# Two layers with causal attention, spectral mixing, channel attention and routed experts: affinities token by row in their own banks, six tiles routed in pairs, first expert weights copied as parts of their buffer come free

## The reference

```python
x = input_features.reshape(-1, D)
aff = jax.lax.stop_gradient(x @ centroids.T)          # 4096 x 8
eid = jnp.argmax(aff, axis=-1)
alpha = jax.nn.sigmoid(jnp.sum(x * centroids[eid], axis=-1, keepdims=True))
xn = (x - mu) * jax.lax.rsqrt(var + EPS)
xln = xn * ln_g[eid] + ln_b[eid]
for e in range(E):                                     # 8 experts, 256 -> 1024 -> 256
    h = jax.nn.relu(xln @ w1[e] + b1[e])
    ffn = ffn + onehot[:, e:e + 1] * (h @ w2[e] + b2[e])
out = x + alpha * ffn
```

## Time and profile before

| | us |
|---|---|
| median of 3 runs | 1555.1 |
| lowest and highest | 1551.25, 1556.09 |
| the profiled execution | 1549.12 |
| its span, first to last instruction | 1547.1 |
| TensorE busy | 1417.8 |
| VectorE busy | 1076.7 |
| ScalarE busy | 854.5 |
| GpSimd busy | 240.9 |

### The profile page before, as it was taken

The page is one execution under the profiler, slowest core; times in us unless marked ns, Lnnn a source line. Parts: engine busy times, 40 slices in busy tenths (PEclk is TensorE's granted clock), DMA queues, the critical chain, the costliest instruction groups (busy, mean ns, idle before and its releaser), DMA issues. The chain is left out here.

```text
span 1547.1 us, 43841 instructions
## 1 busy us (share of the span) xinstructions
PE 1417.8 (92%) x18356; PEld 858.0 (55%) x18356; DVE 1076.7 (70%) x1993; ACT 854.5 (55%) x1783; POOL 240.9 (16%) x380
## 2 busy tenths in 40 slices
PE   7878999999999999999999999898977559999998
PEld 4434444444444444444444453786754259999997
DVE  2376768888887888878888871554558647677675
ACT  2335647767677677676776767552425323433333
POOL 3212021011101111021111110000112611111111
PEclk9999999999999999999999999897998779999999
DMA  8574018513215113142300000570032254554541
GB/s 234 158 120 91 22 64 120 66 26 49 34 28 68 27 30 47 28 59 28 88 3 3 4 2 2 190 257 7 1 98 79 76 208 171 182 186 178 186 175 71
DMA packets 77823, 134.09 MB, mean 87 GB/s; under 512 B 12226, under 2 KB 64443, under 8 KB 72252
## 3 DMA queue, kind: packets, MB, share of 16 engines
q1 hardware_dynamic: 72412, 121.45, 30.4%
q0 software_dynamic: 3408, 8.43, 1.6%
q10 hardware_dynamic: 1808, 1.41, 0.3%
HBM read 67.77 MB, written 23.11 MB: 59 GB/s over the span
## 5 line engine op out<-in xcount | busy, mean ns | idle before, releaser
L1512 DVE TENSOR_REDUCE part_max<-pair 128x2 f32<-128x1024 f32 (+2 forms) x576 | 647.5, 1162 | 115.3 <-PE pair L982 57.4
L1334 ACT ACTIVATE big<-pair 128x512 f32<-128x512 f32 (+1 forms) x1120 | 565.2, 610 | 239.7 <-PE pair L1003 237.4
L976 PE MATMUL pair<-big 128*32 128x512 bf16 (+3 forms) x5120 | 359.6, 352 | 29.1 <-DVE part_max L1512 24.2
L1003 PE MATMUL pair<-big 128*32 128x512 bf16 (+3 forms) x5120 | 345.1, 351 | 3.4 <-issue 1.4
L1025 PE MATMUL pair<-big 128*17 128x512 f32 (+3 forms) x2560 | 280.3, 528 | 2.7 <-issue 2.3
L976 PEld LDWEIGHTS pair<-big 128*32 128x32 bf16 x5120 | 135.1, 97 | 198.4 <-DVE part_max L1512 98.8
L1003 PEld LDWEIGHTS pair<-big 128*32 128x32 bf16 x5120 | 126.8, 96 | 174.3 <-ACT big L1334 88.7
L1347 ACT ACTIVATE std<-moments,eps_col 128x1 f32<-128x1 f32 (+1 forms) x110 | 32.5, 295 | 261.6 <-DVE moments L1550 261.6
L1878 POOL TENSOR_SCALAR_AFFINE_SELECT big<-big 128x512 f32<-128x512 f32 x128 | 80.0, 637 | 474.3 <-ACT big L1334 474.3
L1242 PEld LDWEIGHTS pair<-big,tok 128*128 128x128 f32 x1248 | 147.8, 195 | 4.9 <-DVE big L1778 3.0
L1242 PE MATMUL pair<-big,tok 128*128 128x128 f32 x1248 | 148.3, 278 | 2.4 <-DMA tok<-big 1.4
(11 more groups left out here) (163 smaller groups left out, 1279.0 us busy)
## 6 DMA issues: line engine op xcount, KB each, us to landing
tok<-big SPq DMA_DIRECT2D x39, 1024.0 KB
big<-in_L_ffn_w SPq DMA_DIRECT2D x16, 1024.0 KB, 12.3
big<-split_dram SPq DMA_DIRECT2D x216, 64.0 KB, 4.6
split_dram<-big SPq DMA_DIRECT2D x32, 384.0 KB, 2.7
big<-split_dram SPq DMA_DIRECT2D x42, 256.0 KB, 6.1
big<-routed_dram SPq DMA_DIRECT2D x39, 129.0 KB, 2.1
tok<-in_L_attn_x SPq DMA_DIRECT2D x8, 512.0 KB, 9.2
big<-in_c_query_rows SPq DMA_DIRECT2D x8, 512.0 KB, 5.3
```

Of the source, the lines that this page charges most:

```text
L976: mm = pe.matmul(bank[q:q + STRIPE, o:o + w], m.q_op[slot][:, step.qt, h, step.r * P + q:step.r * P + q + STRIPE], m.k_op[slot][:, h, step ...
L1003: mm = pe.matmul(m.bank[step.bank][k:k + STRIPE, n * w:(n + 1) * w], m.k_op[slot][:, h, step.kb * P + k:step.kb * P + k + STRIPE], m.q_op[ ...
L1334: act.activation(m.p_ring[:, step.place, step.heads[0]:step.heads[-1] + 1, step.at:step.at + w], m.bank[step.bank][:, 0:len(step.heads) * ...
L1512: dve.tensor_reduce(m.part_max[(step.u * QT + step.qt) % 2][:, step.r, step.heads[0]:step.heads[0] + n, step.c], banks[:, :, 0:w], X, ALU. ...
```

## The change

Affinities. For each of the four blocks of a tile the turned tokens are the stationary operand and the centroids are moved, so that the result is token by row, 128 x 8 for a block. It goes to one of two banks of its own (5 and 6), and VectorE reads it there. The copy by ScalarE and the transposes are gone; the product banks are used by products alone. Counts have bank 7.

Routes. The steps Best, Hot, Choose and PlaceRows are made for a route and no more for a tile; a route is one or two tiles (`ROUTES`). A step of two tiles works on 64 values a row in place of 32; its counts take nine small products in place of five. With the rules of the plan the steps behind C5 come as: A1, F4, Best 0; C6, Hot 0; A2, Choose 0; F5, PlaceRows 0; C7; A3; F6, Best 1; A4, Hot 1; F7, Choose 1; A5 (with End of F7 ahead of it), PlaceRows 1; A6, Best 2; Hot 2, A7, Choose 2; PlaceRows 2; and then routes 3 and 4 step by step.

Weights. `scatter` is four semaphores, one for each eight blocks. SP copies the first three weights ahead of the row fetches: copy i waits for the experts' numbers and for the scatters of its own eight blocks, but not for the other scatters, the pads written by ScalarE or the rows.

```diff
+
+ROUTES = [(0, 1), (2, 3), (4, 5), (6,), (7,)]
+SCATTERS = 8
-TURN_BANKS, PRODUCT_BANKS, ROUTE_BANK, FOLD_BANKS = (0, 1), (2, 3, 4), 5, (6, 7)
+TURN_BANKS, PRODUCT_BANKS, FOLD_BANKS = (0, 1), (2, 3, 4), (6, 7)
+AFFINITY_BANKS, COUNT_BANK = (5, 6), 7
...
-            if g and g - 1 not in self.affine_turned:
+            route = next(i for i, tiles in enumerate(ROUTES) if g in tiles)
+            if route >= 2 and route - 2 not in self.made_hot:
                 self.n_job += ROUTE_LAG
-                while g - 1 not in self.affine_turned:
+                while route - 2 not in self.made_hot:
                     take(self.routes, 1)
-            b, added, affine = self.product_bank()
-            self.n_affine += 1
-            self.bank_affine[b] = self.n_affine
-            self.steps.append(Affinity(self.turn_of[stage, g], g, b, added, affine))
+            self.steps.append(Affinity(self.turn_of[stage, g], g, route))
             self.routed[self.turn_of[stage, g]] = g + 1
             self.affine_job[g] = self.n_job
...
     def route_steps(self):
-        for g in range(TILES):
-            while self.affine_job.get(g, self.n_job) + ROUTE_LAG > self.n_job:
+        for route, tiles in enumerate(ROUTES):
+            while self.affine_job.get(tiles[-1], self.n_job) + ROUTE_LAG > self.n_job:
                 yield
-            self.steps.append(Best(g))
-            self.affine_turned.add(g)
+            self.steps.append(Best(route))
             yield
-            self.steps.append(Hot(g))
+            self.steps.append(Hot(route))
+            self.made_hot.add(route)
             yield
-            self.steps.append(Choose(g))
+            self.steps.append(Choose(route))
...
+            self.steps.append(PlaceRows(route, self.norm_of["F", tiles[-1]] + 1))
             yield
...
+        self.affinity = [self.bank[b] for b in AFFINITY_BANKS]
+        self.count_all = self.bank[AFFINITY_BANKS[len(ROUTES) % 2]][:, 0:EXPERTS]
...
         elif isinstance(step, Affinity):
-            slot = step.n % 2
+            slot, tiles = step.n % 2, ROUTES[step.route]
             pe.wait_ge(s.turn_copied, 2 * step.n + 2)
-            if step.added:
-                pe.wait_ge(s.added, step.added)
-            if step.affine:
-                pe.wait_ge(s.affine_copied, step.affine)
             pe.wait_ge(s.params_set, 3)
-            for c in range(KC):
-                mm = pe.matmul(m.bank[step.bank][0:EXPERTS, :], m.cent_t[:, c, :], m.turned_x[slot][:, c, :],
-                               start=(c == 0), stop=(c == KC - 1))
+            if step.route == 1:
+                pe.wait_ge(s.channel_copied, KC * BATCHES)
+            elif step.route >= 2:
+                pe.wait_ge(s.hot_set, step.route - 1)
+            for r in range(BPT):
+                o = ((step.g - tiles[0]) * BPT + r) * EXPERTS
+                for c in range(KC):
+                    mm = pe.matmul(m.affinity[step.route % 2][:, o:o + EXPERTS], m.turned_x[slot][:, c, r * P:(r + 1) * P],
+                                   m.cent_t[:, c, :], start=(c == 0), stop=(c == KC - 1))
             mm.then_inc(s.turn_used, 1)
...
-        elif isinstance(step, Best):
-            g = step.g
-            pe.wait_ge(s.affine_copied, g + 1)
-            if g:
-                pe.wait_ge(s.counts_taken, g)
-            for i in range(BPT):
-                mm = pe.transpose(m.bank[ROUTE_BANK][:, i * EXPERTS:(i + 1) * EXPERTS], m.aff_t[:, i * P:(i + 1) * P],
-                                  m.ident[0:EXPERTS, 0:EXPERTS])
-            mm.then_inc(s.affine_turned, 1)
...
         elif isinstance(step, Hot):
+            i, blocks = step.route, len(ROUTES[step.route]) * BPT
+            n, counts, hot = blocks * EXPERTS, m.bank[COUNT_BANK], m.hot[i % 2][:, 0:blocks, :]
+            pe.wait_ge(s.hot_set, i + 1)
+            pe.wait_ge(s.chosen_set, i + 1)
+            if i == 0:
+                pe.wait_ge(s.onesb_set, 1)
+                pe.wait_ge(s.cbias_set, BATCHES)
+            else:
+                pe.wait_ge(s.counts_taken, i)
+            pe.matmul(counts[:, 0:n], m.before, hot.rearrange("p b e -> p (b e)"), start=True, stop=False)
+            for j in range(blocks - 1):
+                pe.matmul(counts[:, (j + 1) * EXPERTS:n], m.ones_b, wide(hot[:, j, :], [P, blocks - 1 - j, EXPERTS], 1),
                           start=False, stop=False)
+            pe.matmul(counts[:, 0:n], m.ones_b, wide(m.chosen[i % 2], [P, blocks, EXPERTS], 1),
                       start=False, stop=True).then_inc(s.counted, 1)
+    pe.wait_ge(s.chosen_set, len(ROUTES) + 1)
+    pe.matmul(m.count_all, m.ones_b, m.chosen[len(ROUTES) % 2], start=True, stop=True).then_inc(s.counted, 1)
...
-        elif isinstance(step, Affinity):
-            act.wait_ge(s.turn_used, step.g + 1)
-            if step.g:
-                act.wait_ge(s.affine_turned, step.g)
-            act.activation(m.aff_t, m.bank[step.bank][0:EXPERTS, :], ACTF.Copy).then_inc(s.affine_copied, 1)
...
         elif isinstance(step, Best):
+            i, tiles = step.route, ROUTES[step.route]
+            blocks, shape = slice(tiles[0] * BPT, (tiles[-1] + 1) * BPT), [P, len(tiles) * BPT, EXPERTS]
+            affinity = m.affinity[i % 2][:, 0:shape[1] * EXPERTS].rearrange("p (b e) -> p b e", e=EXPERTS)
+            if i == 0:
                 dve.wait_ge(s.channel_in, 128)
                 dve.wait_ge(s.grammed, BATCHES)
+            dve.wait_ge(s.turn_used, tiles[-1] + 1)
+            step_done(dve.tensor_reduce(m.tok[:, blocks, D], affinity, X, ALU.max))
 
         elif isinstance(step, Hot):
+            i, tiles = step.route, ROUTES[step.route]
+            blocks, shape = slice(tiles[0] * BPT, (tiles[-1] + 1) * BPT), [P, len(tiles) * BPT, EXPERTS]
+            affinity = m.affinity[i % 2][:, 0:shape[1] * EXPERTS].rearrange("p (b e) -> p b e", e=EXPERTS)
+            equal, order = m.equal[i % 2][:, 0:shape[1], :], m.order[i % 2][:, 0:shape[1]]
+            step_done(dve.tensor_tensor(equal, affinity, wide(m.tok[:, blocks, D], shape, 2), ALU.is_equal))
+            step_done(dve.tensor_tensor(equal, equal, wide(rank, shape, 1), ALU.mult))
+            step_done(dve.tensor_reduce(order, equal, X, ALU.max))
+            dve.tensor_tensor(m.hot[i % 2][:, 0:shape[1], :], wide(rank, shape, 1), wide(order, shape, 2),
                               ALU.is_equal).then_inc(s.hot_set, 1)
+            dve.wait_ge(s.hot_set, i + 1)
 
         elif isinstance(step, Choose):
+            i, n = step.route, len(ROUTES[step.route]) * BPT
+            step_done(dve.tensor_reduce(m.chosen_g, m.hot[i % 2][:, 0:n, :].rearrange("p b e -> p e b"), X, ALU.add))
+            if i:
+                dve.wait_ge(s.counted, i)
+            dve.tensor_tensor(m.chosen[(i + 1) % 2], m.chosen[i % 2], m.chosen_g, ALU.add).then_inc(s.chosen_set, 1)
+            dve.wait_ge(s.chosen_set, i + 2)
 
         elif isinstance(step, PlaceRows):
+            i, tiles = step.route, ROUTES[step.route]
+            n = len(tiles) * BPT
+            shape, place, row = [P, n, EXPERTS], m.place[i % 2][:, 0:n, :], m.row[i % 2][:, 0:n]
+            dve.wait_ge(s.counted, i + 1)
+            dve.tensor_tensor(place, m.bank[COUNT_BANK][:, 0:n * EXPERTS].rearrange("p (b e) -> p b e", e=EXPERTS),
+                              wide(region, shape, 1), ALU.add).then_inc(s.counts_taken, 1)
+            dve.wait_ge(s.counts_taken, i + 1)
+            step_done(dve.tensor_tensor(place, place, m.hot[i % 2][:, 0:n, :], ALU.mult))
+            step_done(dve.tensor_reduce(row, place, X, ALU.add))
+            dve.tensor_copy(m.position[:, tiles[0] * BPT:(tiles[-1] + 1) * BPT], row).then_inc(s.placed, 1)
+            dve.wait_ge(s.placed, i + 1)
 
...
         elif isinstance(step, PlaceRows):
-            g = step.g
-            pool.wait_ge(s.placed, g + 1)
+            tiles = ROUTES[step.route]
+            pool.wait_ge(s.placed, step.route + 1)
             pool.wait_ge(s.normed, step.normed)
-            for blk in range(g * BPT, (g + 1) * BPT):
+            for blk in range(tiles[0] * BPT, (tiles[-1] + 1) * BPT):
                 pool.indirect_dma_start(m.routed_dram, bass.IndirectOffsetOnAxis(ap=m.position[:, blk:blk + 1], axis=0),
-                                        m.tok[:, blk, :], None).then_inc(s.scatter, 16)
+                                        m.tok[:, blk, :], None).then_inc(s.scatter[blk // SCATTERS], 16)
 
...
+
+    sp.wait_ge(s.expert_set, 1)
+    sp.wait_ge(s.experts_in, 16 * 2 * EXPERTS)
+    for i in range(W1_AHEAD):
+        sp.wait_ge(s.scatter[i], 16 * SCATTERS)
+        fetch_w1(i)
     sp.wait_ge(s.rows_set, 1)
-    sp.wait_ge(s.expert_set, 1)
-    sp.wait_ge(s.scatter, 16 * BLOCKS)
+    for scatter in s.scatter:
+        sp.wait_ge(scatter, 16 * SCATTERS)
     sp.wait_ge(s.pads_out[0], 16 * EXPERTS // 2)
     sp.wait_ge(s.pads_out[1], 16 * EXPERTS // 2)
-    sp.wait_ge(s.experts_in, 16 * 2 * EXPERTS)
     for i in range(ROWS_AHEAD):
```

(2 more changed lines are left out.)

97 lines of the change are left out of this document (26 added, 71 removed).

## The result

The changed kernel takes 1556.59 us (median of 10 runs, 1554.16 to 1560.26); the kernel before, beside it, 1551.35 (1547.96 to 1556.09). The ratio is 1.0035, 95% interval 1.0020 to 1.0049: slower by about 5 us, where 3.6 us faster was forecast.

The account below looks back on a forecast made before the run. The expert stage, bound by TensorE, starts sooner once scatters replace pads as the bound: row fetch 4.0 us sooner, 0.15 won and 0.5 lost on weights, 3.6 us in all, giving 1551.5 us; range 1546.5 to 1557.5.

Parts of the forecast that it names:

- What bounds the kernel: Expert stage: TensorE bounds it at 7.2 to 7.35 us a tile, unchanged; the gain is how much sooner it starts.
- End of F7 at 1210.4: VectorE ahead of route 1's positions: this step comes at 1210.4 in place of 1215.9, 5.5 us sooner.
- The affinity's size: TensorE's affinity of a tile: 1.1 to 1.6 us against 1.88 at full clock, 1.8 to 2.2 against 3.5 at half.
- It never waits again: GpSimd's last 24 scatters: positions always come in time, so they run without waits, 29.1 us from first to last issue.
- The last issue: GpSimd's last scatter: positions of route 1 at 1211.4 plus 29.1 give 1240.5, against 1242.85.
- The pads leave the path: Pad writes ahead of the row fetch: they land before the scatters, winning the 3 us they ended late.
- The weight copies: SP's first three copies, out at 1233.6 to 1235.8: win 0.15 us, cost the row fetch 0.5; last scatter lands after 3.7.
- Rival 2: Hand-over to the experts: weight copies starve scatters and row fetch; only 1.0 us won, 1554.1; chance 0.13.
- Rival 3: Products of C6 and C7: TensorE stays at half clock, VectorE waits; 1.8 to 6 us slower, 1557 to 1561; chance 0.1.

Follow-up runs that it names:

- d_held: The changed kernel with every scatter behind the first route held until all counts are made: one time, 1556.08 us.
- a_oldweights: The changed kernel with the weight copies put back in their old order (row fetch 0, copy 0, row fetch 1, ...): 1551.71 us against 1549.50, ratio 1.0019.
- f_hold_aff: a_oldweights with the third route's scatters held until affinity 7 is signalled: 1550.10 us, ratio 1.0002.
- g_before_long: The kernel before with the scatters of tile 2 held until tile 4's positions are made: one time, 1560.82 us.
- b_single: The changed kernel with eight routes of one tile in place of five, narrow affinities kept: 1559.95 us, ratio 1.0069.

## Why the prediction was wrong

- **What bounds the kernel** held. The expert stage kept its 7.2 us a tile, and 6.7 of the 7.2 us between the two profiled executions are the moment at which it starts.
- **End of F7 at 1210.4**: 1211.84. Positions of route 1 were to be there at 1211.4 and were at 1212.85. Part of this nearness is luck: 5.5 us were to be saved, and 3.9 were, of which the changed code made 3.0 (3.0 to 3.7 over the traces with doubled routes, counted from C4). VectorE waited 2.73 and 0.97 us for C7's product, where 2.1 us of lateness was forecast. The affinity's size was wrong: 1.85 us at full clock and 3.42 at half (16 passes), not 1.1 to 1.6 and 1.8 to 2.2; the old form has 1.88 and 3.54. The nearest row had been four passes with a small loaded operand; here each pass loads 128 x 128, and the 16 loads fill the time (1.86 and 3.49 us on the weight-load track). It was left out of the sum as lying beside VectorE's work, but two of them stand in the chain of the pads, below. The doubled instructions start 0.25 to 0.26 us apart, as taken.
- **"It never waits again"** is the step that failed. It came from VectorE's and TensorE's own durations, with positions of route 3 nine us behind those of route 1; they came 23.8 us behind (1236.64 against 1212.85). The durations alone would not have broken it: without scatters beside them, in d_held, the positions of routes 2, 3 and 4 were there 8.2, 11.7 and 14.1 us behind those of route 1, in time for scatters that need 10, 20 and 25. What broke it is the silent premise that GpSimd's issues cost other engines nothing. No row supported it, and the trace of before had a sign against it: affinity 6 ends at 1223.15 and is signalled at 1225.31, and the next counts end at 1224.01 and are signalled at 1227.45, beside the only run of eight scatters (1216.89 to 1226.69):

```profile
1227.54 0.19 DVE L1723 TENSOR_TENSOR acc_t<-pair,small 128x32 f32<-128x32 f32 x1 [3.43 <-remote]
```

The prediction booked the following gap of 1.96 as a wait for VectorE's work. The last issue: forecast 1240.5, measured 1246.04. The 5.5 us are 1.7 for the later start of the run, 3.6 for the gap and 0.3 for one stretched scatter.

- **"The pads leave the path"** fell with it: addresses at 1239.34 and not 1223. Behind the shift of F7 they came 27.5 us later, where 12.5 were forecast. In d_held, without scatters beside the routing, it was 15.4: so 12.1 us are the late signals', and 2.9 the chain's own, which was costed too low. From the turn of A7 to the end of affinity 7 TensorE was put at 5.5 us and took 8.9 (1214.51 to 1223.41), with two affinities of 3.4 to 3.6 us.
- **The weight copies** were put at 1233.6 to 1235.8, done long before the rows. They went out at 1247.48 and cost 1.2 us ahead of the fetch (6.3 us from last issue to fetch, 5.1 in a_oldweights, 4.6 forecast; the last scatter landed 4.5 us behind its issue, 3.7 forecast) and 3.9 of landing (6.0 us against 2.1). The price was in the list of bounds (0 to 1.7 for the landing) but too small: the row behind it showed rows behind one copy, and here there are three. That they stay ahead of the rows when they come late was not considered; it is written in SP's order. Rival 2 had copies that hold up scatters and rows, but on the way to a gain of 1.0 us.
- **Rival 3**, the clock, half came true: it stayed at half from 1202 on, and F7 was 3.9 us ahead nevertheless. A loss of 5 us lies in this rival's bracket (1.8 to 6), but it came by another mechanism.

In sum, against the forecast in the trace: the last scatter is issued 5.5 us late, of which 3.6 are GpSimd's gap; the fetch follows it 1.7 us later than forecast, and the rows land 3.3 us later than forecast. The copies' share of the loss, by a_oldweights, is about 5. With the copies put back and the stop cut short (f_hold_aff) the kernel is at the old time, 0.3 us over by the ratio, not 3.6 under. Of that distance GpSimd's gap is 2.0 (2.33 less the usual 0.30), and the later start of the run, 1.7 us in the changed kernel's trace, is most of the rest.

## What to carry to other kernels

An engine's unbroken run of indirect scatters can have a price on other engines that no duration shows; when a change joins two such runs, look in the old trace for waits that end long after the work they wait for ("remote"), and price the joined run by them. When transfers are put ahead of the urgent one on a queue because they "will be early", ask what happens when what releases them comes late: the order stays, the head start doesn't. A gain ahead of a chain is worth only what the next thing on that chain lets through.

## What the runs showed of the hardware

- Beside 16 gapless scatters of 128 rows TensorE's signals (affinities and counts alike) came up to 11.7 us late, with 1 KB rows and with 128-byte rows alike; in the changed kernel the two longest held came 1.2 and 2.6 us behind the end of the run. Beside runs of eight the latest signal was 1.5 to 3.9 us late, and beside 12, in the old code, 5.6; beside runs of four, and beside 22 us of memsets, none was. The first signals over 1 us late came 4 to 8 us into a run. Length isn't all: in g_before_long and b_single long runs went on while signals were 0 to 2.7 us late. TensorE's records show the work itself as taken up in time, and VectorE's signals to TensorE came through (hot rows at 1223.5, counting products at 1223.78). Why it is TensorE's that are held, and what else than the run it takes, no run shows.
- SP's four pads took 4.0 to 8.5 us to issue in most runs, 13.4 in b_single and 18.0 in g_before_long, always with scatters beside them. What sets this, no run shows.
- Sixteen passes of 128 fp32 columns by 8 took 1.85 us at the full clock and 3.42 at half, as long as their loads of 128 x 128 (1.86 and 3.49). Rows fetched behind 3 MB of copies, on the same queue (q1), were used 5.6 to 6.1 us behind their fetch, against 2.1 to 2.3 in the traces where no copy was issued directly ahead. The Trainium skill (DMA: Bandwidth & Descriptors, Queues, rings and completion order) says that each engine goes round between queues a packet at a time; that bears on the scatters, which have a queue of their own (q0), and no run here isolates it.
